# A graph attention layer in split float32: the attention's projections, scores and values in 64-row matmuls, two at a time on the halves of the rows

## What is computed

```python
h = jnp.maximum(_layernorm(x, axis=-1), 0.0)
q = h @ wq.T + bq;  k = h @ wk.T + bk;  v = h @ wv.T + bv
q2 = (q @ wiq.T + biq).reshape(N, H, D).transpose(1, 0, 2)
k2 = (k @ wik.T + bik).reshape(N, H, D).transpose(1, 0, 2)
v2 = (v @ wiv.T + biv).reshape(N, H, D).transpose(1, 0, 2)
scores = jnp.einsum('hnd,hmd->hnm', q2, k2) * scale + mask[None]
attn = jax.nn.softmax(scores, axis=-1)
out = jnp.einsum('hnm,hmd->hnd', attn, v2)
return x + (out.transpose(1, 0, 2).reshape(N, OUT_F) @ wo.T + bo)
```

## Time and profile before

| what | value |
|---|---|
| time, median of 3 runs | 294.5 us (294.37 to 294.74) |
| span of the profiled execution | 292.6 us |
| busy, PE (matmul) | 286.9 us, 98% |
| busy, VectorE | 176.3 us, 60% |
| busy, ScalarE | 153.7 us, 53% |
| busy, GpSimd | 149.9 us, 51% |
| granted TensorE clock, mean | 1.00 |

### The profile page before, as it was taken

How to read it: one execution, slowest core, us unless ns; L and a number is a source line. 1 busy time by engine, 2 the same in 40 slices (tenths; PEclk the granted TensorE clock), 3 DMA queues, 4 the chain that set the end, 5 groups by cost and what they waited for, 6 DMA issues and landing times.

```text
span 292.6 us, 4992 instructions
## 1 busy us (share of the span) xinstructions
PE 286.9 (98%) x1809; PEld 266.0 (91%) x1809; DVE 176.3 (60%) x473; ACT 153.7 (53%) x289; POOL 149.9 (51%) x156
## 2 busy tenths in 40 slices
PE   6999999999999999999999999999999999999996
PEld 3799998888899999999999999999999997888885
DVE  4999878696534543454377676665748475835241
ACT  2986343242542344234434685969687879774100
POOL 6452454453454544644400796748393939873000
PEclk9999999999999999999999999999999999999999
DMA  7969965839643344324454043040403122400032
GB/s 269 324 237 266 330 219 165 249 113 341 222 143 106 112 144 146 116 100 146 164 212 146 0 147 119 26 147 0 146 23 124 50 97 72 146 0 0 2 143 72
DMA packets 15818, 40.84 MB, mean 140 GB/s; under 512 B 3481, under 2 KB 4914, under 8 KB 15794
## 3 DMA queue, kind: packets, MB, share of 16 engines
q1 hardware_dynamic: 13346, 38.53, 39.6%
q0 software_dynamic: 2016, 1.21, 1.5%
q10 hardware_dynamic: 432, 0.79, 0.7%
HBM read 37.71 MB, written 2.81 MB: 138 GB/s over the span
## 4 chain that ended last, share of the span: by engine, by line
PE 96%; DMA 1%; DVE 1%; ACT 0%; POOL 0%; issue 0%
PE banks L884 27%; PE banks L885 26%; PE banks L886 26%; PE banks L1015 5%; PE banks L1058 3%; PE banks L1059 3%; PE banks L1030 3%; PE banks L1043 1%; DMA x_sb<-in_x 1%; PE banks L935 1%; DVE stats L711 1%; PE banks L975 1%; PE banks L965 0%; PE banks L978 0%; ACT x_sb L504 0%; POOL rstd L384 0%
## 5 line engine op out<-in xcount | busy, mean ns | idle before, releaser
L426 POOL DMA_INDIRECT cells<-value,cell x51 | 54.5, 1069 | 60.2 <-DMA cells<-value,cell 47.5
L479 ACT ACTIVATE w_hi<-raw 128x1024 fp32r<-128x1024 f32 x50 | 52.6, 1053 | 19.5 <-PE banks L886 17.3
L886 PE MATMUL banks<-a_lo,w_hi 128*128 128x384 f32 x184 | 61.5, 334 | 0.0
L884 PE MATMUL banks<-a_hi,w_hi 128*128 128x384 f32 x184 | 61.5, 334 | 0.0
L885 PE MATMUL banks<-a_hi,w_lo 128*128 128x384 f32 x184 | 61.5, 334 | 0.0
L747 DVE TENSOR_TENSOR w_lo<-raw,w_hi 128x1024 fp32r<-128x1024 f32 x36 | 44.2, 1229 | 12.4 <-ACT w_hi L479 12.2
L452 POOL TENSOR_SCALAR prob<-prob,row_inv 128x384 f32<-128x384 f32 x36 | 22.6, 645 | 42.6 <-DVE row_inv L814 42.6
L884 PEld LDWEIGHTS banks<-a_hi,w_hi 128*128 128x128 f32 x184 | 34.5, 188 | 0.0
L885 PEld LDWEIGHTS banks<-a_hi,w_lo 128*128 128x128 f32 x184 | 34.5, 188 | 0.0
L886 PEld LDWEIGHTS banks<-a_lo,w_hi 128*128 128x128 f32 x184 | 34.5, 188 | 0.0
L399 POOL TENSOR_TENSOR w_lo<-raw,w_hi 128x1024 fp32r<-128x1024 f32 x14 | 33.7, 2410 | 0.0
(11 more groups left out here) (151 smaller groups left out, 611.0 us busy)
## 6 DMA issues: line engine op xcount, KB each, us to landing
raw<-in_slabs SPq DMA_DIRECT2D x56, 512.0 KB, 3.4
work<-key_rows SPq DMA_DIRECT2D x6, 256.0 KB, 5.6
prob<-key_rows SPq DMA_DIRECT2D x6, 256.0 KB, 3.9
x_sb<-in_x SPq DMA_DIRECT2D x3, 512.0 KB, 5.2
out_y<-x_sb SPq DMA_DIRECT2D x5, 256.0 KB, 2.1
cells<-prob SPq DMA_DIRECT2D x2, 576.0 KB, 7.6
cells<-value,cell POOLq DMA_INDIRECT x51, 3.7
x_sb<-in_x ACTq DMA_DIRECT2D x3, 256.0 KB, 4.4
```

The source lines that it names most:

```text
L426: nc.gpsimd.indirect_dma_start(out=cells[c][:, :], out_offset=bass.IndirectOffsetOnAxis(ap=cell[:, t:t + 1], axis=0), in_=value[:, t:t + 1 ...
L479: nc.scalar.activation(split_place(s)[0], raw[:, s % RAW, :], ACT.Copy).then_inc(slab_hi, 1)
L884: nc.tensor.matmul(psum, w[0], a[0], start=first, stop=False)
L886: return nc.tensor.matmul(psum, w[0], a[1], start=False, stop=last)
```

## The change

The array's two halves of 64 rows are now used for everything from the pairs' projections on, until the output projection:

- **Query and key projections.** q and k are computed in blocks of 64 + 64 features (slabs of wq and wk are loaded in turn, `slab_source`, and interleaved as they are split, `raw_place`, `split_place`), so that partitions 0 to 63 of every `b` and `c` tile hold q and 64 to 127 hold k. A pair's q2 and k2 then come from 48 steps (`pair_steps`) of two 64-row matmuls, q2 on the lower and k2 on the upper rows, into two banks.
- **Values.** The rows of v2 and of the turned probabilities are laid out in blocks of 64, one head on each half, and `pair_values` does both heads at once in 12 steps of two 64-row matmuls, into banks 6 and 7. v2's parts are copied out of PSUM in quarters (24 copies for 6 on ScalarE and on VectorE).
- **Banks.** Scores and turns share banks 0 to 3 (`score_place`: 0/1, 2/3, 0/1; `turn_place`: 2/3, 0/1, 2/3); projections use 4 and 5 (pair 1: 6 and 7). All pairs are turned with 64-row transposes, a third of a pair at a time (`turn(pair, m)`), and converted 768 wide, three a pair instead of six.
- **Order.** Written anew on PE, ScalarE, VectorE and GpSimd: projection of the pair after next in pieces between scores and turns; one round per pair. Reciprocals are taken two at a time. Some early buffers share storage.

```diff
+SLABS_OF_STEP = [((37 + 2 * j,), (38 + 2 * j,)) for j in range(PAIRS - 1)] + [((51, 52), (53,)), ((54, 55), ())]
...
             for j in range(PAIRS + 1):
-                first, second = slabs_of_step(j) if j < PAIRS else ((), ())
-                h = 2 * (j - 1)
+                first, second = SLABS_OF_STEP[j]
+                if 2 <= j < PAIRS:
+                    pair_hi_part(j - 2)
+                for s in first:
+                    split_hi(s)
                 if j < PAIRS:
-                    exp_part(j, 0)
-                    exp_part(j, 1)
-                if in_halves(h):
-                    exp_part(j, 2)
-                    for s in first:
-                        split_hi(s)
-                    tile_hi_part(3 * KT + 3 + 2 * j)
-                if j >= 2:
-                    half_part(h - 1)
+                    for n in range(NT):
+                        exp_part(j, n)
                 if j >= 1:
-                    for m in range(NT):
-                        pt_hi_part(h, m)
-                if j >= 2:
-                    pair_hi_part(j - 2)
-                if in_halves(h):
-                    for s in second:
-                        split_hi(s)
-                    if j >= 1:
-                        for m in range(NT):
-                            pt_hi_part(h + 1, m)
-                        half_part(h)
-                    if j < PAIRS - 2:
-                        tile_hi_part(3 * KT + 4 + 2 * j)
-                else:
-                    for s in first:
-                        split_hi(s)
-                    half_part(h)
-                    if j < PAIRS:
-                        exp_part(j, 2)
-                    for m in range(NT):
-                        pt_hi_part(h + 1, m)
-                    for s in second:
-                        split_hi(s)
-            half_part(H - 1)
+                    for m in range(2):
+                        pt_hi_part(j - 1, m)
+                if j == PAIRS:
+                    pair_hi_part(PAIRS - 2)
+                if j >= 1:
+                    pt_hi_part(j - 1, 2)
+                if j < PAIRS - 1:
+                    for second_of in range(2):
+                        tile_hi_part(3 * KT + 2 * (j + 1) + second_of)
+                for s in second:
+                    split_hi(s)
+                if j >= 1:
+                    half_part(j - 1)
             pair_hi_part(PAIRS - 1)
...
             for j in range(PAIRS + 1):
-                h = 2 * (j - 1)
                 if j < PAIRS:
-                    for n in range(NT):
-                        max_part(j, n)
-                if j == 0:
-                    y_part(0)
-                if j < PAIRS:
+                    max_part(j, 0)
+                    if j == 0:
+                        y_part(0)
+                    max_part(j, 1)
                     inv_part(j, 0)
-                if j == 0:
-                    y_part(1)
-                if j < PAIRS:
+                    if j == 0:
+                        y_part(1)
+                    max_part(j, 2)
                     inv_part(j, 1)
-                if j == 0:
-                    y_part(2)
-                if in_halves(h):
+                    if j == 0:
+                        y_part(2)
                     inv_part(j, 2)
-                    tile_lo_part(3 * KT + 3 + 2 * j)
-                if j >= 2:
-                    head_part(h - 1)
                 if j >= 1:
-                    for m in range(NT):
-                        pt_lo_part(h, m)
+                    for m in range(2):
+                        pt_lo_part(j - 1, m)
                 if j == PAIRS:
                     pair_lo_part(PAIRS - 2)
-                if in_halves(h):
-                    if j >= 1:
-                        for m in range(NT):
-                            pt_lo_part(h + 1, m)
-                        head_part(h)
-                    if j < PAIRS - 2:
-                        tile_lo_part(3 * KT + 4 + 2 * j)
-                else:
-                    head_part(h)
-                    if j < PAIRS:
-                        inv_part(j, 2)
-                    for m in range(NT):
-                        pt_lo_part(h + 1, m)
-            head_part(H - 1)
+                if j >= 1:
+                    pt_lo_part(j - 1, 2)
+                if j < PAIRS - 1:
+                    for second_of in range(2):
+                        tile_lo_part(3 * KT + 2 * (j + 1) + second_of)
+                if j >= 1:
+                    head_part(j - 1)
             pair_lo_part(PAIRS - 1)
...
+            def pair_steps(pair, first, end):
+                if first == 0:
+                    pe.wait_ge(v2_lo, 4 * GS * NT)
+                    if pair >= 1:
+                        pe.wait_ge(tile_lo, 3 * KT + (0, 0, 2, 6)[pair] if pair < 4 else 3 * KT + 2 * pair)
+                for step in range(first, end):
+                    half, k, p = step // STEPS, step % STEPS // 3, step % 3
+                    s, block_at = QK0 + 2 * pair + half, 2 * k + half
+                    if step == first or step % STEPS == 0:
+                        hi, lo = split_slab(s)
+                    if pair == 0 and p == 0:
+                        pe.wait_ge(tile_lo, KT + block_at + 1)
+                    a_h, a_l = (b_hi, b_lo) if block_at < KT else (c_hi, c_lo)
+                    w, a = ((hi, a_h), (lo, a_h), (hi, a_l))[p]
+                    for x in range(2):
+                        own, _ = rows_of(x)
+                        mm = nc.tensor.matmul(bank[pair_place(pair) + x][:, 0:N], w[own, k * P:(k + 1) * P],
+                                              a[own, block_at % KT, :], start=(step == 0), stop=(step == 2 * STEPS - 1))
+                    if step % STEPS == STEPS - 1:
+                        mm.then_inc(slab_used, 1)
...
             def scores(j, n):
-                turn, m = j % 2, slice(n * P, (n + 1) * P)
-                if j >= 2:
-                    pe.wait_ge(pt_lo_ok, (2 * j - 3) * NT + n + 1)
+                m, at = slice(n * P, (n + 1) * P), score_place(n)
                 if n == 0:
-                    pe.wait_ge(tile_lo, 3 * KT + 2 * j + 2)
-                    if j >= 1:
-                        pe.wait_ge(masked, chunk_at(j - 1, NT - 1, 1) + 1)
+                    pe.wait_ge(tile_lo, 3 * KT + 2 * (j + 1))
+                if n == 2:
+                    pe.wait_ge(masked, chunk_at(j, 0, 1) + 1)
+                elif j >= 2:
+                    pe.wait_ge(pt_lo_ok, turn_at(j - 2, n + 1) + 1)
+                elif j == 1:
+                    pe.wait_ge(masked, chunk_at(0, (2, 1)[n], 1) + 1)
                 for p, (q, k) in enumerate(((q2_hi, k2_hi), (q2_hi, k2_lo), (q2_lo, k2_hi))):
...
+            def turn(pair, m):
+                at, j = turn_place(m), pair + 1
+                if m == 0:
+                    pe.wait_ge(prob_ok, chunk_at(pair, NT - 1, 1) + 1)
+                if m == 2:
+                    pe.wait_ge(pt_lo_ok, turn_at(pair, 0) + 1)
+                elif j < PAIRS:
+                    pe.wait_ge(masked, chunk_at(j, m + 1, 1) + 1)
+                else:
+                    pe.wait_ge(pt_lo_ok, turn_at(pair - 1, 2 - m) + 1)
+                for b in (2 * m, 2 * m + 1):
...
+                            columns = prob[own, pair % 2, n, b, :, :].rearrange("p x d -> p (x d)")
+                            mm = nc.tensor.transpose(bank[at + high][:, to:to + D], columns, ident[own, own])
+                            if n == NT - 1:
+                                mm.then_inc((pt_done, pt_done_high)[high], 1)
...
+            def pair_values(pair):
+                if pair >= 1:
+                    pe.wait_ge(head_sum, 2 * pair)
+                else:
+                    pe.wait_ge(tile_lo, 3 * KT + 4)
+                order = [(b, p) for b in range(4) for p in range(2)] + [(b, p) for p in range(2) for b in (4, 5)]
+                for i, (b, p) in enumerate(order):
+                    pe.wait_ge((pt_hi_ok, pt_lo_ok)[p], turn_at(pair, b // 2) + 1)
...
+            pair_steps(0, 0, 2 * STEPS)
+            pair_steps(1, 0, FIRST_STEPS)
+            scores(0, 0)
+            pair_steps(1, FIRST_STEPS, 30)
+            scores(0, 1)
+            pair_steps(1, 30, 40)
+            scores(0, 2)
+            pair_steps(1, 40, 48)
+            pair_steps(2, 0, 8)
+            for j in range(1, PAIRS - 1):
+                scores(j, 0)
+                pair_steps(j + 1, 8, 16)
+                scores(j, 1)
+                pair_steps(j + 1, 16, 24)
+                scores(j, 2)
+                pair_steps(j + 1, 24, 32)
+                turn(j - 1, 0)
+                pair_steps(j + 1, 32, 38)
+                turn(j - 1, 1)
+                pair_steps(j + 1, 38, 42)
+                turn(j - 1, 2)
+                pair_steps(j + 1, 42, 48)
+                pair_values(j - 1)
+                if j < PAIRS - 2:
+                    pair_steps(j + 2, 0, 8)
...
+            last = PAIRS - 1
```

(30 more changed lines are left out.)

459 lines of the change are left out of this document (215 added, 244 removed).

## The result

| | time, median | profiled span | mean granted clock |
|---|---|---|---|
| before | 294.44 us (294.22 to 294.74) | 292.6 | 1.00 |
| after | 376.06 us (375.05 to 377.24) | 374.2 | 0.90 |

What follows compares the result with a forecast made beforehand. PE's own stream (96% of the chain) bounds the kernel; -5.0 us of stream savings plus +7.2 of waits gave +2.2, so 296.7 us against 294.5, with 8 in 10 runs from 292.5 to 299.4.

Steps and rivals of the forecast that it cites:

- slab pairs are split 4 us ahead: Slab supply throughout: listed as covered and put at no wait; a late slab would cost its lateness once.
- The stream that can't be fed (B): Rival for PE's 64-row pairs: four instructions a slot make 0.22 us, +22 us, about 319 us; chance 0.05.
- Two at a slot: PE's matmuls: two 64-row matmuls side by side take one 0.174 us slot, like one 128-row matmul.
- visits: PE passages into 64-row work and back: 0.41 us for scores, 0.35 for turns; fewer visits gain 3.5 us.
- the form: 64-row work on PE: fewer visits 3.5 and cheaper last turns 1.6 lead the -5.0 us sum, if nothing waits.
- the 0.4 of visits that should lie under waits: Changed kernel's six visits cost 2.3 us; about 0.4 of it was counted as hidden under waits, leaving 1.9.
- Conversions: 768-wide copies out of PSUM: 0.81 us on ScalarE (bounds 0.49, 0.98), 0.96 on VectorE (0.55, 1.10).
- The ties: Steady rounds: turn(·, 2) and next pair's projection each wait for low parts ending when PE is due; six each, +1.3 us.
- The other tie: Steady rounds: turn(·, 2) waits for turn(·, 0)'s low part, seen at 4.38 with PE due at 4.39; 0.11 us each.
- The first step: scores(1, 0) waits for pair 1's low parts, held up by maxima and residual sums on VectorE: +1.3 us.
- The value copies have two tiles' time: Value copies on ScalarE and VectorE: 24 quarters for 6 whole ones on each, counted as covered.
- The end: Last pairs: PE waits +2.4 at turn(6, 2), +1.15 at turn(7, 2), +0.85 at k = 6; with 0.2, 4.6 us.

Runs made afterwards that it cites:

- the last kernel: Changed kernel with two loads a slab, plus moved value copies, residual sums, last slabs and end splits, and 14 instead of 8 early pair 2 steps: 291.65 us.
- the kernel with two loads: Changed kernel, but slabs 32 to 47 each loaded by two transfers of 64 rows instead of one from [2, 64, 1024]: 303.16 us, ratio 1.029.

## Why the prediction was wrong, step by step

- **The loads.** The step that failed is the wait for slabs, put at nothing: "slab pairs are split 4 us ahead" stands in the list of what has cover, and a late slab would cost its lateness once. The forecast took the 56 transfers as they were, though the diff changes the source of 16 of them. What the runs showed in its place: a slab comes every 9.97 us where PE uses one in 4.2 to 6.7, so the lateness is paid again with each slab, ScalarE waits 84.8 us for loads, and the load's source alone is worth 72.9 of the 81.6 us. No rival had it. The stream that can't be fed (B) was the nearest in size, but from another cause and wrong in itself: slots of pairs stay at 0.1735 wherever slabs are there.
- **Two at a slot, and visits.** Right: 0.1735 a slot, 0.40 to 0.45 a visit, and the kernel without waits gains. Two loads of 128 columns in 0.1735 also holds against the rule that the forecast weighed and left for its row (the Trainium skill, TensorE: Matmul & The Clock Gate, section LDWEIGHTS (loading the stationary operand), by which two in a row would take 0.213). The size of the gain was too large. Without waits the form is worth 2.8 us (294.44 - 291.65), not 5.0. PE of the last kernel, a third of a turn and the steps behind it:

```profile
184.04 0.53 PE L1111 MATMUL banks<-ident,prob 64*128 64x64 f32 x11
...
184.63 0.40 PE L1070 MATMUL banks<-b_hi,w_hi 64*128 64x384 f32 x2
```

  From 184.04 to 184.63 pass 0.59 for 12 transposes and one slot, so a third costs 0.42, 1.26 a pair, where the forecast had 1.12 and no price for going from transposes back to steps: 8 x 0.14 = 1.1; and the 0.4 of visits that should lie under waits aren't hidden when nothing waits. The rest, 0.7, is about the tie that this kernel still has, 0.9 (below).
- **Conversions.** The 768-wide ones were taken at 0.81 and 0.96 by slope. Right; lines of the kernel after (count, busy us, mean ns, idle before):

```profile
L882 DVE TENSOR_TENSOR pt_lo<-banks,pt_hi 128x768 fp32r<-128x768 f32 x24 | 22.3, 954 | 12.6 <-ACT pt_hi L646 12.6
...
L646 ACT ACTIVATE pt_hi<-banks 128x768 fp32r<-128x768 f32 x24 | 18.5, 800 | 9.5 <-PE banks L1104 9.5
```

- **The ties.** Six of each were priced 0.11, together 1.3 us; one of the two is there. The next pair's projection waits for this pair's last low part. VectorE and PE of the kernel with two loads:

```profile
178.58 0.61 DVE L792 SCALAR_TENSOR_TENSOR k_lo<-banks,bias,k_hi 128x384 fp32r<-128x384 f32 x1
178.87 0.52 PE L1125 MATMUL banks<-pt_lo,v 64*128 64x384 f32 x4
179.29 0.44 PE L1068 MATMUL banks<-b_hi,w_hi 64*128 64x384 f32 x2
179.54 0.37 PE L1068 MATMUL banks<-b_hi,w_lo 64*128 64x384 f32 x2
```

  The low part ends at 179.19, 2.06 after the start of the values at 177.13 (forecast 2.05). PE starts 0.10 behind that end, 0.07 behind its beat, and its slot takes 0.25 and not 0.17: 0.15 in all. The five rounds lose 0.13 to 0.17 each and scores(7, 0), which wait for a low part in the same way, 0.13: 0.9 together, where six of 0.11 are 0.7. That PE starts 0.10 behind the low part's end in every round speaks for the wait and against a price of the change from values to steps; no run separates the two. The other tie cost nothing:

```profile
188.00 0.96 DVE L887 TENSOR_TENSOR pt_lo<-banks,pt_hi 128x768 fp32r<-128x768 f32 x1 [0.61 <-ACT pt_hi L651]
189.07 0.54 PE L1109 MATMUL banks<-ident,prob 64*128 64x64 f32 x11
```

  The chain from scores(j, 2), here at 184.57, took 4.39 (forecast 4.33), but with thirds of a turn at 0.42 PE was due only 4.49 after it, and started on its beat. A round takes 13.4 us (180.75 to 194.18), 0.4 less than the 13.84 before.
- **The first step.** Right in size by accident (1.04 for 1.3), wrong in its cause: not the sums on VectorE but 8 slots against a hand-over of 2.5 us. In the steady step the same chain had 12 and 8 slots, and the forecast counted it only there.
- **"The value copies have two tiles' time".** Wrong: 12 copies of 0.38 and 0.42 us instead of 3 of 0.6 and 0.69 are 5 us on each engine, over twice as much, ahead of tile 8's parts: 1.8 us.
- **The end.** turn(6, 2) 2.42 for 2.4 and turn(7, 2) 1.46 for 1.15: right, and by the cause that was named, ScalarE's slabs. k = 6 was 2.12 for 0.85: the port shared with GpSimd. And the clock, for which the sum had no term, adds 3.1.

With its own terms corrected the sum holds: -2.8 for the form (with the tie in it), +8.8 of waits and +3.1 of clock are +9.1; measured with two loads a slab +8.7. On top of that lies the load's 72.9.

## What to carry to other kernels

A change to what a tensor holds on which partition is a change to its load: look at the shape of both sides of every transfer that the diff touches, not only at bytes and row length. A load that gathers two blocks is better made as two transfers of one block each: 303.16 us against 376.06 here. A profile on which the DMA share stands still at 1/8 (2 of 16 engines) while ScalarE waits for loads is this case. In an order written by hand, a wait of some us costs twice: once as idle, and, behind most of the waits of 2.4 us and more here, as the clock that falls after it.
